# Layer 1: the residual rows of the first normalisation made by ACT instead of Pool

## The reference, cut to what matters

```python
x = _layernorm(x + _L1_attn_ref(x, ...), axis=-1)      # the first normalisation
x = _layernorm(x + _L1_ffn_ref(x, ...), axis=-1)

def _L1_ffn_ref(x, ...):
    mu, var = mean(x), var(x)                            # per token
    z = (x - mu) * rsqrt(var + EPS) * ln_g + ln_b
    z_bn = (mean(z, axis=1) - bn_mean) * rsqrt(bn_var + EPS) * bn_g + bn_b
    probs = softmax(z_bn @ Wr + br); idx = argmax(probs); gate = probs[idx]
    h = relu(z @ W_down[idx] + b_down[idx])              # one expert for a whole sequence
    y = h @ W_up[idx] + b_up[idx]
    return y * gate
```

## Time and profile before

| | |
|---|---|
| median of 3 runs | 1584.42 us |
| lowest, highest | 1584.26, 1594.23 us |
| the profiled execution | 1600.77 us, span 1599.0 us |
| mean granted TensorE clock | 0.925 |
| PE busy | 1333.7 us (83%) |
| DVE busy | 952.3 us (60%) |
| ACT busy | 609.2 us (38%) |
| Pool busy | 277.4 us (17%) |
| chain that ended last, by engine | PE 31%, DVE 9%, issue 2%, ACT 1%, Pool 1% |

### The profile page before, as it was taken

One profiled execution on the slowest core, in us unless ns is written; L12 is line 12 of the kernel. 1 busy time (PEld: TensorE's weight loads), 2 busy tenths in 40 slices (PEclk: granted clock), 3 DMA queues, 4 the chain that ended last, 5 costly groups with the idle time before them and its releaser, 6 DMA issues. The chain is left out here.

```text
span 1599.0 us, 25207 instructions
## 1 busy us (share of the span) xinstructions
PE 1333.7 (83%) x8819; PEld 831.2 (52%) x8819; DVE 952.3 (60%) x2373; ACT 609.2 (38%) x1152; POOL 277.4 (17%) x294
## 2 busy tenths in 40 slices
PE   4488888888888889739995699899989898989864
PEld 1234444444544455439995455656555555555532
DVE  3365666665666657227777365666666767676642
ACT  0034444444443445315552134344344344434331
POOL 2111120212111200111112121021222222212022
PEclk9799999999999999859998689999999999999975
DMA  3432614141414132524211424404040404040000
GB/s 109 121 102 68 164 55 115 61 100 61 100 61 100 48 90 83 170 76 163 70 61 40 130 73 106 100 21 126 21 116 31 116 32 117 31 104 1 15 14 13
DMA packets 68235, 127.40 MB, mean 80 GB/s; under 512 B 8320, under 2 KB 58128, under 8 KB 64656
## 3 DMA queue, kind: packets, MB, share of 16 engines
q1 hardware_dynamic: 65040, 117.39, 26.8%
q0 software_dynamic: 3072, 8.41, 1.7%
HBM read 84.32 MB, written 40.66 MB: 78 GB/s over the span
## 5 line engine op out<-in xcount | busy, mean ns | idle before, releaser
L533 DVE TENSOR_REDUCE first_maxima<-bank 128x1 f32<-128x512 f32 (+3 forms) x352 | 220.4, 638 | 212.9 <-PE bank L346 209.7
L482 ACT ACTIVATE arena<-pair 128x512 f32<-128x512 f32 x320 | 187.2, 596 | 318.1 <-PE pair L375 315.6
L1308 ACT ACTIVATE second_probs<-pair 128x512 f32<-128x512 f32 (+1 forms) x256 | 137.5, 541 | 300.1 <-PE pair L1173 292.0
L1458 DVE TENSOR_REDUCE second_maxima<-bank 128x2 f32<-128x512 f32 (+1 forms) x224 | 153.8, 688 | 143.5 <-PE bank L1149 141.9
L343 PE MATMUL bank<-stacks 96*128 96x256 bf16 (+3 forms) x512 | 126.8, 304 | 46.6 <-DVE first_maxima L533 25.0
L324 PE MATMUL bank<-first_xT,w_qkv 128*128 128x512 f32 x256 | 135.6, 660 | 9.7 <-DVE first_halves L518 5.5
L368 PE MATMUL pair<-stacks 99*128 99x512 bf16 (+3 forms) x512 | 124.3, 304 | 17.0 <-DMA stacks<-first_m_turned 14.7
L1147 PE MATMUL bank<-second_k_stack,second_q_stack 96*128 96x256 bf16 (+1 forms) x512 | 90.4, 269 | 7.7 <-DMA second_k_stack<-parked 6.2
L1170 PE MATMUL pair<-second_q_stack,second_k_stack 99*128 99x256 bf16 (+1 forms) x512 | 94.4, 266 | 0.6 <-ACT second_probs L1308 0.6
L1173 PE MATMUL pair<-logits,constants_bf 128*128 128x512 bf16 (+1 forms) x256 | 93.7, 366 | 0.0
L343 PEld LDWEIGHTS bank<-stacks 96*128 96x128 bf16 x512 | 44.3, 98 | 93.4 <-DVE first_maxima L533 45.2
(11 more groups left out here) (324 smaller groups left out, 2417.5 us busy)
## 6 DMA issues: line engine op xcount, KB each, us to landing
stacks<-parked SPq DMA_DIRECT2D x96, 256.0 KB, 6.7
parked<-first_parts SPq DMA_DIRECT2D x32, 384.0 KB, 2.7
parked<-second_parts SPq DMA_DIRECT2D x32, 384.0 KB, 2.5
second_q_stack<-parked SPq DMA_DIRECT2D x48, 256.0 KB, 5.2
second_k_stack<-parked SPq DMA_DIRECT2D x48, 256.0 KB, 8.1
expert_xs<-sorted_x SPq DMA_DIRECT2D x39, 128.5 KB, 2.1
sorted_y<-expert_ys SPq DMA_DIRECT2D x39, 128.0 KB, 1.7
first_xT<-in_xT SPq DMA_DIRECT2D x8, 512.0 KB, 4.1
```

What stands on the lines that cost most here:

```text
L482: act.activation(PT[:, s:s + len(heads), lo:lo + each], ex[n % 3][:, 0:len(heads) * each].rearrange("p (h q) -> p h q", h=len(heads)), ACT ...
L533: dve.tensor_reduce(nm[:, i, qt, heads[0]:heads[0] + len(heads)], mx[n % 2][:, 0:wide].rearrange("p (h k) -> p h k", h=len(heads)), AX.X, ...
L1308: act.activation(PT[:, s:s + len(heads), lo:lo + each], ex[n % 2][:, 0:len(heads) * each].rearrange("p (h q) -> p h q", h=len(heads)), ACT ...
L1458: dve.tensor_reduce(nm[:, i, qt, heads[0]:heads[0] + len(heads)], mx[n % 2][:, :].rearrange("p (h k) -> p h k", h=len(heads)), AX.X, ALU.m ...
```

## The change

The four `new_x` items of a sequence go from Pool to ACT, at the same places of the list. Pool computed `(x - mean) * rstd`, ACT computes `rstd * x + bias`. The bias, minus mean times `rstd[:, 0]`, is four columns that DVE computes in `nb`, ahead of what it did there, into the first four columns of `lrec`. The schedule, the waits for `z` and the count of `new` stay.

```diff
@@ ACT
+                    elif kind == "new_x":
+                        if i == 0:
+                            act.wait_ge(lp["z"], 2 * (b + 1))
+                        act.activation(x[:, i, :], x[:, i, :], ACT.Identity, bias=lrec[:, i:i + 1], scale=rstd[:, 0, i:i + 1])\
+                            .then_inc(lp["new"], 1)
@@ DVE
                     elif kind == "nb":
                         dve.wait_ge(lp["rstd"], b + 1)
+                        dve.scalar_tensor_tensor(out=lrec[:, 0:NT], in0=mv[:, :, 0], scalar=-1.0, in1=rstd[:, 0, :],
+                                                 op0=ALU.mult, op1=ALU.mult)
                         dve.scalar_tensor_tensor(out=nb[:, :], in0=mv[:, 0:2, 0], scalar=-1.0, in1=rstd[:, 1, 0:2],
                                                  op0=ALU.mult, op1=ALU.mult).then_inc(lp["nb"], 1)
@@ Pool
-                    elif kind == "new_x":
-                        if i == 0:
-                            pool.wait_ge(lp["z"], 2 * (b + 1))
-                        pool.tensor_scalar(x[:, i, :], x[:, i, :], mv[:, i, 0:1], rstd[:, 0, i:i + 1], ALU.subtract, ALU.mult)\
-                            .then_inc(lp["new"], 1)
```

## The result

| | before | after |
|---|---|---|
| median (runs) | 1585.78 us (4) | 1621.89 us (4) |
| ratio | | 1.018, 95% interval 1.014 to 1.022 |
| profiled execution, span | 1600.77, 1599.0 us | 1625.45, 1623.7 us |
| mean granted clock of that execution | 0.925 | 0.913 |

What follows compares the result with a forecast made beforehand. The prediction took PE's hole before the router's matmul, fed by ACT's queue, as the bound. 11.0 us of delay plus 3.6 of clock drops gave 14.6 us, 1584.4 + 14.6 = 1599 us; range 1588 to 1608.

Steps and rivals of the forecast that it cites:

- What bounds the stretch: Before the router's matmul L1227: PE has a hole, waiting for DVE's copy L1529, fed by ACT's queue, in all eight sequences.
- Pool's removal worth 0, the copy faster: 41.6 us off Pool gain nothing themselves; copy L1529 takes 0.29 us everywhere, in all -1.5 us.
- DVE's operation: One four-column operation ahead of nb makes nb 0.08 us later, hidden in sequences 0 to 4, counted in the last three.
- The delay on ACT: Four activations ahead of z_in 1 make it 1.57 us late; router's matmul 1.31 us late in sequences 0 to 4.
- the replay: ACT's queue around one normalisation, recomputed item by item with the four new activations: z_in 1 comes 1.57 us late.
- its four terms 6.6, 1.5, 2.0 and 0.9: Delays in us of the router's matmul: sequences 0 to 4 together, then 5, 6 and 7; together 11.0.
- I take three drops in seven, 3.6 us: Behind the longer PE holes before L1227: clock halves in three of seven sequences, 1.2 us each.
- the bound of 11.9: Upper bound in us for the clock term: seven drops at 1.7 us each.
- the rows of 2.31 us of waiting: At 1431.3 us PE had waited 2.31 us for DVE; the clock then fell to 0.50.
- rows 10: Profile rows near 1431 to 1433 us showing a clock drop to 0.50 for some 3.4 us.
- Rival 1: Clock drops in nearly every sequence at the hole before L1227: over 1% slower, with all seven 1604 to 1607 us; chance 0.41.
- Rivals 2 and 3: 2: PE's later waits shrink and hide the delay, +3 us, chance 0.06. 3: Pool's absence wins, 1582 us, chance 0.05.

Runs made afterwards that it cites:

- ACT twice: Kernel before, Pool keeping its new_x, with four extra 128x256 activations a sequence on ACT into unread scratch columns: ratio 1.0187, median 1629.98 us.
- ACT late: Changed kernel with ACT's four new_x moved behind z_in 1: ratio 1.0009, median 1605.78 us.
- changed again: The repeated comparison: the unaltered changed kernel run once more beside the kernel before: ratio 1.0162, median 1625.43 us.
- the filled kernels: Useless matmuls put in PE's hole ahead of the router's matmul: six in the changed kernel, ratio 1.0047; five in the kernel before, 0.9963.
- Pool late: Kernel before with Pool's new_x listed behind zb, which left Pool doing the rows at the same time: ratio 1.0002.
- ACT half: Changed kernel with two new_x of a sequence ahead of z_in 1 and two moved behind: ratio 1.0033, median 1604.05 us.

## Why the prediction was wrong

- **What bounds the stretch**: right. The chain ran DVE, L1227; ACT's queue fed it, without room.
- **Pool's removal worth 0, the copy faster**: right in effect. Nobody waited for Pool. The copy went to 0.29 us in all sequences. But ACT twice shows that the delay alone brings this. The cause given for the 0.53 us (held until Pool's operation is through) fits the copies that end just behind a boundary between two `new_x`, but not the one of sequence 6, which takes 0.29 us inside a `new_x`. So that the later of the two waits for the whole instruction, with which the prediction had the trace agree, is borne out by some of its rows and not by that one; the profile's spans on Pool are rough, and the cause has not been isolated.
- **DVE's operation**: right; ACT late contains it and is not slower than before.
- **The delay on ACT**: right, to a few hundredths. `z_in` 1 came 1.53 us late (1.57 in the replay), L1227 1.26 (1.31). The sum of 11.0 us met 10.2 in the rows (6.3, 1.35, 1.8 and 0.7 for its four terms 6.6, 1.5, 2.0 and 0.9), 12 us at equal clock in the repeated comparison and 8 between the filled kernels.
- **The clock, "I take three drops in seven, 3.6 us"**: this is the term that failed. The drops came behind six and seven of seven holes and cost 11.3 and 16.9 us in the rows, the second above even the bound of 11.9 that I had put on it. All three factors were too small. The count: the replay had the hole nearly right (0.68 and 1.42 us of waiting with a score group between; 2.1 in all, where I wrote 2.5), but I counted that group as a protection, and the rows of 2.31 us of waiting were the near ones to go by. The length: one of the drops in the first profile and four of the seven in the repeated one last 6.8 us, where I took 3.4 for all, as in rows 10. The price: a drop of 3.4 us costs 1.64 to 1.69 us in sequences 0 to 5, the full price of 1.7, and not 1.2; that these matmuls "lose less" did not show. The first profile of the changed kernel also has more at half clock elsewhere, three stretches of 10 to 17 us behind the experts' matmuls instead of one of 10 (some 4.5 us of time for each 10). The repeated profile and ACT twice have one each, like before, and lose as much, so these stretches are not needed for the loss.
- **Rival 1** is what happened, with its mechanism and place. It came out, so a chance of 0.41 for over 1% looks low in hindsight; its own 19 to 23 us and 1604 to 1607 were too low as well, by the drops' length. Rivals 2 and 3 fell: no later wait took back the delay.
- **The median** also played a part: the first comparison's runs of before lay near 1586 us, those of the other jobs near 1602, and the profiled 1600.8 with 0.925 was the usual case. Put on 1602 the forecast would have been some 1617 us, against 1625 measured; it is the same term that falls short.

## What to carry to other kernels

Moving work from an idle engine to another with idle time costs what it delays in the receiving queue: replay that queue, item by item, up to the next thing that the bounding engine waits for. If it lengthens a hole of TensorE (here from 1.2 to 2.1 us), price the halved clock behind the hole as well, at half the length of the drop where the engine is full; here that was 11 to 17 us, more than the delay of 10. Place the moved work behind the critical item, and, where a hole must stay, a few matmuls without use inside it can be worth more than they cost (1.2 to 1.4% in the changed kernel; nothing in ACT late, whose hole had no drop behind it).

## What the runs showed of the hardware

- TensorE's clock went to 1.2 GHz behind holes of 2.1 us in two pieces (changed, changed again and ACT twice: six, seven and seven of seven) and 2.8 us in one (seven of seven). It did not behind those of 1.2 us in before and Pool late or of 0.9 us in ACT late (none of seven each; sequence 6 has a wait of 0.62 us more ahead), but it did behind one of 1.1 us in two pieces in ACT half. The Trainium skill ("TensorE: Matmul & The Clock Gate", HAM oscillation) tells of a kernel that falls back to the slow clock in every wait for its next tile. The runs here agree that a wait repeated in each round can cost its clock in nearly each, and show more: it need not be in one piece, with a score group of matmuls between.
- A drop of 3.4 us right behind the hole, with PE full, cost 1.64 to 1.69 us over the same matmuls (sequences 0 to 5), one of 6.8 us 3.1 to 3.3. Over whole executions a microsecond at half clock went with 0.38 us of time (77 runs).
- Before the experts' output PE idles 0.6 us while it reads the expert's number; three matmuls issued ahead of that read fill the gap (0.81 us of work), and neither of the two profiles with them has a long stretch of half clock behind this place in the first six sequences. Without them the other profiles have none to three, so two profiles are thin evidence; the 24 and 26 us less at half clock in the means support it.
- PE can be full and stay at half clock: in before it was busy 10.00 of 10.00 us over 1152.60 to 1162.60 at 0.50.
